# A Mamba-style layer between two feed-forward layers: scan tiles of 2 states x 64 channels instead of 4 states x 128 channels

## The reference, cut to what matters

```python
h  = layernorm(layernorm(x)) * norm_w + norm_b
xz = h @ Win;  x_ssm, z = split(xz, 2)          # 512 channels each
x_ssm = silu(conv4(x_ssm) + conv_b)
dt = softplus(x_ssm @ dt_w + dt_b);  A = -exp(A_log)
Bt = x_ssm @ Bp;  Ct = x_ssm @ Cp               # 64 states each
def step(state, inp):                           # over 512 tokens
    dA = exp(dt_t[:, :, None] * A[None])
    state = state * dA + (dt_t * x_t)[:, :, None] * B_t[:, None, :]
    y_t = einsum('bds,bs->bd', state, C_t)
y = (ys + x_ssm * D) * silu(z)
out = x + y @ Wout
```

## Time and profile before

| | |
|---|---|
| median of 3 runs | 6116.61 us |
| profiled execution, own time | 6156.25 us |
| its span | 6154.4 us |
| PE matmul busy | 5423.4 us (88%), 86664 instructions |
| POOL busy | 5101.6 us (83%) |
| DVE busy | 4829.4 us (78%) |
| ACT busy | 4068.8 us (66%) |
| mean granted TensorE clock | 0.948 of full |
| DMA packets, bytes | 650457, 1095.40 MB |

### The profile page before, as it was taken

One profiled execution on the slowest core, in us unless ns is written; L12 is line 12 of the kernel. 1 busy time (PEld: TensorE's weight loads), 2 busy tenths in 40 slices (PEclk: granted clock), 3 DMA queues, 4 the chain that ended last, 5 costly groups with the idle time before them and its releaser, 6 DMA issues.

```text
span 6154.4 us, 207624 instructions
## 1 busy us (share of the span) xinstructions
PE 5423.4 (88%) x86664; PEld 3375.6 (55%) x86664; DVE 4829.4 (78%) x4323; ACT 4068.8 (66%) x6785; POOL 5101.6 (83%) x2326
## 2 busy tenths in 40 slices
PE   5888889888898988899888998888988889898887
PEld 2455555555565555555555565555655556555554
DVE  0679787787887878788787887878778788797996
ACT  3767576666766667576675766657666676766664
POOL 0779798887988879798797988979888798897996
PEclk9899999999999999999999999999999999999999
DMA  5566665666656666666665656656566666655553
GB/s 132 199 153 222 145 212 171 169 202 153 208 156 188 202 157 208 155 187 199 161 209 150 197 194 157 210 143 209 176 170 206 148 213 156 190 189 142 191 179 112
DMA packets 650457, 1095.40 MB, mean 178 GB/s; under 512 B 302817, under 2 KB 336386, under 8 KB 583938
## 3 DMA queue, kind: packets, MB, share of 16 engines
q1 hardware_dynamic: 649474, 1081.40, 60.9%
HBM read 875.74 MB, written 205.52 MB: 176 GB/s over the span
## 4 chain that ended last, share of the span: by engine, by line
POOL 52%; issue 23%; PE 10%; SPq 6%; DMA 5%; DVE 1%; ACT 1%; POOLq 1%; DVEq 0%; ACTq 0%
POOL H L602 49%; SPq L303 6%; DMA Cb<-scratch_c 4%; PE pUB L687 3%; PE Y L713 3%; DVE H L567 1%; POOL lnv L616 1%; POOL dto L620 1%; PE pP L642 1%; PE pP L648 1%; SPq L289 1%; PE pP L635 1%; POOLq L601 0%; DMA Bd<-scratch_diag 0%; POOL X L626 0%
## 5 line engine op out<-in xcount | busy, mean ns | idle before, releaser
L567 DVE TENSOR_TENSOR_SCAN H<-dA,pUB 128x512 f32<-128x512 f32 x4096 | 4698.3, 1203 | 1108.8 <-PE pUB L687 1061.6
L602 POOL TENSOR_TENSOR H<-H,Cb 128x1024 f32<-128x1024 f32 x2048 | 4814.8, 2387 | 824.1 <-DVE H L567 815.7
L435 ACT ACTIVATE dA<-DT,w_negA 128x512 f32<-128x512 f32 x4096 | 2615.3, 710 | 1134.5 <-DVE H L567 1121.6
L687 PEld LDWEIGHTS pUB<-Bd,UT 64*64 64x64 f32 x65536 | 1975.6, 136 | 1560.5 <-issue 1547.5
L687 PE MATMUL pUB<-Bd,UT 64*64 64x128 f32 x65536 | 2303.3, 277 | 556.5 <-DMA Bd<-scratch_diag 247.1
L713 PE MATMUL Y<-H,w_ident 64*64 64x512 f32 x16384 | 2026.9, 605 | 69.4 <-POOL H L602 63.1
L713 PEld LDWEIGHTS Y<-H,w_ident 64*64 64x64 f32 x16384 | 660.6, 137 | 658.2 <-issue 649.4
L435 ACT ACT_TABLE_LOAD x224 | 287.4, 1283 | 4.0
L408 ACT ACTIVATE absv<-pP,w_dt_b 128x512 f32<-128x512 f32 x64 | 44.0, 687 | 358.3 <-PE pP L648 358.3
L635 PE MATMUL pP<-hT,w_Win 128*128 128x512 f32 x512 | 264.4, 641 | 16.0 <-ACT uto L423 12.7
L648 PE MATMUL pP<-U,w_dt_w 128*128 128x512 f32 x512 | 270.9, 655 | 3.4 <-ACT zo L399 3.4
(11 more groups left out here) (85 smaller groups left out, 2350.3 us busy)
## 6 DMA issues: line engine op xcount, KB each, us to landing
Cb<-scratch_c SPq DMA_DIRECT2D x512, 1024.0 KB, 5.5
Bd<-scratch_diag SPq DMA_DIRECT2D x512, 512.0 KB, 4.5
scratch_diag<-blank SPq DMA_DIRECT2D x512, 256.0 KB, 5.9
scratch_z<-zo SPq DMA_DIRECT2D x64, 256.0 KB, 6.3
scratch_dt<-dto SPq DMA_DIRECT2D x64, 256.0 KB, 6.4
scratch_ut<-uto SPq DMA_DIRECT2D x64, 256.0 KB, 7.4
DT<-scratch_dt SPq DMA_DIRECT2D x64, 256.0 KB, 5.3
UT<-scratch_ut SPq DMA_DIRECT2D x64, 256.0 KB, 6.6
```

The source lines that it names most:

```text
L435: last = nc.scalar.activation(dA[:, n % DAR, j, :], DT[:, k, :], ACT.Exp, scale=c["negA"][:, k, GS * blk + j:GS * blk + j + 1])
L567: last = nc.vector.tensor_tensor_scan(H[:, n % HR, 2 * i + j, :], dA[:, n % DAR, 2 * i + j, :], pUB[:, i, :].rearrange("p (t s) -> p s t", ...
L602: nc.gpsimd.tensor_tensor(h[:, j:j + 2, :], h[:, j:j + 2, :], Cb[:, blk % 2, j:j + 2, :], ALU.mult).then_inc(times_c, 1)
L687: last = nc.tensor.matmul(out, UT[rows, k, j * P + h * HP:j * P + h * HP + HP], Bd[rows, blk % 2, i, j * P:(j + 1) * P].rearrange("p (t s) ...
```

## The change

The unit keeps its size (128 partitions x 4 scans x 512), but a partition now stands for one of 64 channels and one of two pairs of states. The four quarters of 32 partitions are (channels 0-31, states 0-1), (channels 0-31, states 2-3), (channels 32-63, states 0-1), (channels 32-63, states 2-3). The four scans of a unit are two channel tiles (`j // 2`) by two states (`j % 2`). So:

- `force` makes 32 matmuls for a half unit (4 x 4 quarters x 2), with 32 weights' columns and 128 moving columns each, in 64x32 tiles, where there were 16 in 64x64 tiles.
- `add_states` is one call for each pair, placed behind `force(n+1, 1)` at even n. Its weights `sel` are four 32x32 identities below one another, so the product over 64 partitions adds the two pairs of states. A pair takes 16 matmuls of 512 columns in 64x32 tiles, where it took two calls of 8 in 64x64 tiles.
- `skip_over` takes 8 matmuls of 128 rows x 32 columns twice per sequence instead of 2 of 64x64 four times. It moves to n = 2 and 34.
- `Cb` needs 2 rows of C for each partition instead of 4, so its load halves. C is stored twice, dt is stored twice, and `DT` is loaded at twice the size.
- `store_diagonals` stores one of 8 parts a unit, n = 25 to 32, each 64 partitions x 16 pieces of four numbers.
- The setup loads `A_log` in 32 small transfers instead of 1, and `Win`, `Wout` in 32 pieces instead of 16.

```diff
-SPS = {... "store B": (25,), ...
+SPS = {... "store B": (25, 26, 27, 28, 29, 30, 31, 32), ...
...
+            rates = w["A_log"].rearrange("(q r i) (b p t) -> r p q i b t", q=2 * KI, r=2, b=NBLK, p=2)
+            small += [(alog[(2 * r + par) * QP:(2 * r + par + 1) * QP, q, :].rearrange("p (b t) -> p b t", t=2), rates[r, par, q])
+                      for r in range(2) for par in range(2) for q in range(2 * KI)]
...
+            link(nc.vector.tensor_tensor(c["sel"][:, :], c["ident"][:, 0:QP], c["ident"][:, QP:2 * QP], ALU.add))
+            for part in (2, 3):
+                link(nc.vector.tensor_tensor(c["sel"][:, :], c["sel"][:, :], c["ident"][:, part * QP:(part + 1) * QP], ALU.add))
...
-                rows = dram["c"][bass.ds(b, 1), GS * blk + 1:GS * (blk + 1) + 1, :].rearrange("o s t -> o (s t)")
-                sp.dma_start(Cb[:, seq % 2].rearrange("p s t -> p (s t)"), rows.to_broadcast([P, GS * T])).then_inc(c_in[seq % 2], 16)
+                rows = dram["c"][bass.ds(b, 1), 2 * GS * blk + 1:2 * GS * (blk + 1) + 1, :].rearrange("o (p s) t -> p (o s t)", p=4)
+                rows = rows.unsqueeze(1).to_broadcast([4, QP, 2 * T])
+                sp.dma_start(Cb[:, seq % 2].rearrange("p s t -> p (s t)"), rows).then_inc(c_in[seq % 2], 16)
...
+                j, r = part // 2, part % 2
+                    lo = EL + r * HP * 2 * T + j * HP * GS
+                    spot = dram["diag"][bass.ds(q, 1), lo:lo + NBLK * 2 * EL].rearrange("o (i x) -> (o i) x", x=2 * EL)
+                    spot = spot[:, 0:HP * (2 * T + GS)].rearrange("i (p x) -> p i x", x=2 * T + GS)[:, :, 0:GS]
+                    sp.dma_start(spot, BT[r * HP:r * HP + HP, j, :].rearrange("p (i s) -> p i s", s=GS)).then_inc(d_st, 16)
...
+                for par in range(2):
+                    sp.dma_start(rows[par], dto[:, :]).then_inc(dt_st, 16)
...
-                            last = nc.scalar.activation(dA[:, n % DAR, j, :], DT[:, k, :], ACT.Exp,
-                                                        scale=c["negA"][:, k, GS * blk + j:GS * blk + j + 1])
+                            last = nc.scalar.activation(dA[:, n % DAR, j, :], DT[:, k, j // 2, :], ACT.Exp,
+                                                        scale=c["negA"][:, 2 * k + j // 2, 2 * blk + j % 2:2 * blk + j % 2 + 1])
...
-                            nc.gpsimd.tensor_tensor(h[:, j:j + 2, :], h[:, j:j + 2, :], Cb[:, blk % 2, j:j + 2, :], ALU.mult).then_inc(times_c, 1)
+                            nc.gpsimd.tensor_tensor(h[:, j:j + 2, :], h[:, j:j + 2, :], Cb[:, blk % 2], ALU.mult).then_inc(times_c, 1)
...
-                    for r in range(2):
-                        rows = slice(r * HP, r * HP + HP)
-                        for h in range(2):
-                            side = slice(h * HP, h * HP + HP)
-                            out = pUB[side, i, r * T:(r + 1) * T].rearrange("p (t j s) -> p j t s", j=NJ, s=2)[:, j]
-                            last = nc.tensor.matmul(out, UT[rows, k, j * P + h * HP:j * P + h * HP + HP],
-                                                    Bd[rows, blk % 2, i, j * P:(j + 1) * P].rearrange("p (t s) -> p t s", s=2),
+                    for quarter in range(4):
+                        ch = j * P + i * HP + quarter // 2 * QP
+                        for r in range(2):
+                            rows = slice(r * HP, r * HP + HP)
+                            out = pUB[quarter * QP:(quarter + 1) * QP, i, r * T:(r + 1) * T].rearrange("p (t j s) -> p j t s", j=NJ, s=2)[:, j]
+                            last = nc.tensor.matmul(out, UT[rows, k, ch:ch + QP],
+                                                    Bd[rows, blk % 2, j, :, quarter % 2 * 2:quarter % 2 * 2 + 2],
                                                     start=True, stop=True)
...
+            def add_states(b, n):
+                pe.wait_ge(times_c, at(2 * (GN * b + n + 2)))
                 pe.sem_inc(pe_go, 1)
+                for j in range(2):
+                    for q in range(4):
+                        for r in range(2):
+                            rows = slice(r * HP, r * HP + HP)
+                            last = nc.tensor.matmul(Y[r][q * QP:(q + 1) * QP, :], c["sel"][rows, :], H[rows, (n + q // 2) % HR, q % 2 * 2 + j, :],
+                                                    start=False, stop=(n % HALF == HALF - 2 and j == 1))
+                last.then_inc(summed, 2)
...
-                    if n % 2:
-                        other(b, n, close, proj, ffn)
-                    if scan and n % 2 == 0 and n:
-                        add_states(b, n - 2, 1)
+                    other(b, n, close, proj, ffn)
+                    if scan and n % HALF == 2:
+                        skip_over(b, n // HALF)
                     if scan and n + 1 < GN:
                         force(b, n + 1, 1)
-                    if n % 2 == 0:
-                        other(b, n, close, proj, ffn)
-                    if scan and n % 2:
-                        add_states(b, n - 1, 0)
+                    if scan and n % 2 == 0 and n:
+                        add_states(b, n - 2)
```

More of the change, by code:

```diff
@@ L14 @@
 HP = P // 2
+QP = P // 4
 GS = 4
@@ L101, in _ @@
                 sp.dma_start(dst, src).then_inc(k_big, 16)
-            for k in range(KI):
-                for r in range(2):
[L104 to L110, removed]
+            for tile in range(KI):
+                for q in range(4):
+                    side, ch = q * QP, tile // 2 * 2 * P + q * HP + tile % 2 * QP
+                    sp.dma_start(c["Win"][:, :, DI + tile * P + side:DI + tile * P + side + QP],
+                                 w["Win"][:, DI + ch:DI + ch + QP].rearrange("(k p) m -> p k m", p=P)).then_inc(k_big, 16)
+                    sp.dma_start(c["Wout"][side:side + QP, tile, :], w["Wout"][ch:ch + QP, :]).then_inc(k_big, 16)
+            sp.wait_ge(k_big, (4 + 8 * KI) * 16)
+            sp.wait_ge(k_small, (10 + 8 * KI) * 16)
         @block.gpsimd
@@ L120, in _ @@
         def _(act):
[L121 removed]
+            act.wait_ge(k_small, (10 + 8 * KI) * 16)
             nc.scalar.activation(wabs[:, :, :], wk[:, :, :], ACT.Abs).then_inc(k_abs, 1)
@@ L698, in skip_over @@
                 pe.sem_inc(pe_go, 1)
                 for r in range(2):
-                    rows, side = slice(r * HP, r * HP + HP), slice(k % 2 * HP, k % 2 * HP + HP)
-                    last = nc.tensor.matmul(Y[r][side, :], c["diagD"][rows, k, rows], U[rows, k, :] if k < 2 else U2[rows, k - 2, :],
-                                            start=True, stop=False)
-                last.then_inc(skip, 1)
-            def add_states(b, n, half):
-                pe.wait_ge(times_c, at(2 * (GN * b + n + 1) + half + 1))
-                pe.sem_inc(pe_go, 1)
-                for j in (2 * half, 2 * half + 1):
-                    for r in range(2):
-                        rows = slice(r * HP, r * HP + HP)
-                        for i in range(2):
-                            last = nc.tensor.matmul(Y[r][i * HP:i * HP + HP, :], c["ident"][rows, rows], H[rows, (n + i) % HR, j, :],
-                                                    start=False, stop=(n % HALF == HALF - 2 and j == GS - 1))
-                if half:
-                    last.then_inc(summed, 2)
+                    for q in range(4):
+                        k, lo = 2 * pr + q // 2, q % 2 * HP + r * QP
+                        last = nc.tensor.matmul(Y[r][q * QP:(q + 1) * QP, :], c["diagD"][:, k, lo:lo + QP],
+                                                U2[:, k - 2, :] if pr else U[:, k, :], start=True, stop=False)
@@ L833, in step @@
                         force(b + 1, 0, 1)
-                    if n % 2 == 0:
-                        other(b, n, close, proj, ffn)
-                    if scan and n % HALF == 1:
-                        skip_over(b, n - 1)
-                        skip_over(b, n)
-                    if scan and n % 2:
-                        add_states(b, n - 1, 0)
+                    if scan and n % 2 == 0 and n:
+                        add_states(b, n - 2)
+                    if close and n == 0:
+                        add_states(b - 1, GN - 2)
             steps(pe, step)
```

74 lines of the change are left out of this document (36 added, 38 removed).

## The result

The changed kernel takes **6300.7 us** (median of 4 runs, 6260.7 to 6324.4) for 6118.3 us of the kernel before beside it: a ratio of 1.0292, 95% interval 1.0234 to 1.0351. The forecast was 5570 us, with 5420 to 5860 as its range. The profiled execution took 6285.92 us.

What follows compares the result with a forecast made beforehand. POOL was taken to set the floor: 318.7 us busy plus 16.3 idle make 335 a sequence; 229.5 + 15 x 335 + 349 = 5603.5 us of span, 5605 own time, times 0.9936 gives 5570 us, range 5420 to 5860.

Steps and rivals of the forecast that it cites:

- the array step: On TensorE, a round of tiles costs its columns, not its instructions: 107 ns for eight tiles in `force`.
- Rivals 3 and 4: Eight tiles don't run side by side, 7470 us, chance 0.05; matmuls are paced one by one, 6600 us, chance 0.03.
- The first scan: End of the setup: added small transfers make the first scan come 32 us later, at 229.5 us.
- A store: Diagonal stores on SP: with half the pieces, each takes 1.5 us of SP, one a unit.
- The long stall on `Bd`: The wait for the load of `Bd` behind eight diagonal stores goes: -16.7 us a sequence.
- `Cb` at half size ... all far ahead of their use: 0: Loads and stores of `Cb`, C, dt and `DT`: all far ahead of their use, cost 0.
- `force`: 32 instructions become 64, in 8 rounds as before: 0: `force` calls on TensorE: twice the instructions in the same 8 rounds cost 0.
- rival 2: TensorE is late through instructions or clock: 22 us a sequence, 5900 us, range 5650 to 5950, chance 0.20.
- 1.1 + 1.9 + 1.1 = 4.1 us fit into 4.5 ... Cost 0: Later place of `add_states` between two `force` calls: cost 0, up to 0.5 us a pair if POOL lags.
- all shapes on ACT, DVE and POOL at 0: ACT, DVE and POOL run the same instructions with the same shapes: cost 0.

Runs made afterwards that it cites:

- e1: The kernel before with only the eight diagonal stores spread, one a unit at n = 25 to 32: 5955.66 us, ratio 0.972.
- e3: The changed kernel with the C rows loaded in four transfers of 32 partitions instead of one: 6030.79 us, ratio 0.9859.
- e8: The kernel of e5 with the C rows in one transfer of 2 x 64 x 1024 instead of two: 7318.52 us, ratio 1.1958.
- e5: The changed kernel laid out in halves of 64 channels, tiles 64 wide or more, C rows in two transfers, C and dt stored once: 6342.11 us, ratio 1.0363.
- e4: The changed kernel with its force products in 64x64 tiles, part of the products wrong: 5962.04 us, ratio 0.9733.
- e13: The kernel of e1 with a one-token matmul added ahead of each force matmul, tiles as before: 7141.52 us, ratio 1.1671.
- e6: The changed kernel with the edits of e3 and e4 together, part of the products wrong: 5752.02 us, ratio 0.9404.
- e14: The kernel of e3 with the Y sum ahead of the second force call, other pieces of even units behind it: 6077.17 us, ratio 0.9928.
- e9: The kernel of e1 with the diagonals stored in pieces of four numbers: 5913.44 us, ratio 0.9664.
- e12: The kernel of e1 with two long-fulfilled semaphore waits ahead of each force matmul: 6458.44 us, ratio 1.0543.

## Why the prediction was wrong

*Right, nearly:* the array step. A round with eight tiles costs little more than one with four did (an undisturbed call of 64 takes 1.19 us, 1.1 forecast), and the Y sum's busy time is 1112.3 us (about 1030 forecast). Over all 2048 calls, the broken ones and those at half clock among them, `force` is busy 2711.3 us for 2303.3. Rivals 3 and 4 are out. The first scan comes at 231.0 us (229.5 forecast). A store takes SP 0.69 us, less than half of the 1.5 forecast. The long stall on `Bd` is gone; spreading alone was worth 166 us or 11 a sequence (e1) for the 16.7 forecast, as part of the wait moved to unit 32.

*The term "`Cb` at half size ... all far ahead of their use: 0"* failed, and cost 270 us (e3 undoes it). I counted bytes, not how many DMA engines carry them. In the 5 us shown above the 16 engines are busy 0.23 of their time, 3.7 engines, at 69 GB/s. At that rate 512 KB take 7.6 us of a pair's 9.3, and the next `Bd` stands behind them: it lands after 6.6 us instead of 4.5. With the outermost dimension at 2 (e8) 2.2 engines are busy and it costs 976 us, and transfers of one row to 32 or 64 partitions each (e3, e5) leave no wait of POOL on `Cb`. The cause is thus the transfer's shape. The Trainium skill ("DMA: Bandwidth & Descriptors", Why a DMA increments its semaphore by 16 and not by 1) says that a transfer uses as many engines as the largest number up to 16 that divides the slowest dimension, other than 1, of both its patterns: 4 here (4 and 128), 2 in e8 (2 and 128). The 3.7 and the 2.2 agree. Had I weighed that rule, the term would not have been 0.

*The term "`force`: 32 instructions become 64, in 8 rounds as before: 0"* failed too, and cost up to 339 us (e4 undoes it, with the wider tiles). It priced the array and left the longer list at nothing: that was rival 2's mechanism, to which I gave 0.20. Rival 2's price for it, 22 us a sequence or 330 in all, agrees with the 339 in the sum only, and that is partly luck: I had put 0.3 us on each of 75 blocks of instructions, and what came is about 24 late ones a sequence of 1.3 us each. What misled me was the earlier trace rows, 62 waits over a whole run: they were too few to look dear, and I took the price of a block for a flat one. It is not flat. Of the blocks that come every 7.9 us 1 in 12 was late (63 waits to 726 packets), and of those every 4.5 us about 3 in 10 are (384 to 1237, each 1.3 us in the mean). The late ones fall into `force`, the densest part of the list (64 matmuls in 1.19 us, for the Y sum's 32 in 1.99), and DVE waits for it. e13 shows the pauses with the tiles unchanged; that it is the block's arrival that ends them rests on their times beside queue 8. The Trainium skill ("Runtime: NRT & Kernel Launch", Instruction fetch mechanics) calls the crossing of a 16-KB block "mostly hidden"; here 509 us of TensorE's idle time aren't, and the measurement decides.

*The rest, 5752 - 5570 = 182 us,* is there even without both causes (e6): 345 us a full sequence for 335, 319 the last one for 298.6 (in its profiled execution, 30 us above its median). The one other place that was tried for the Y sum isn't better (e14). For the last sequence the step can be named: "1.1 + 1.9 + 1.1 = 4.1 us fit into 4.5 ... Cost 0", said of a force call, the Y sum and the force call that DVE needs next. From e6, the last sequence and 14 us of it, and the timeline there:

```profile
5403.50:5722.50 319.00, 242.94 (x5139) 158.58 (x5133) 288.25 (x258) 171.54 (x280) 294.69 (x128) 0.90 0.38 116
5562.00:5576.00 14.00, 11.20 (x224) 6.80 (x220) 12.83 (x12) 7.41 (x12) 13.13 (x6) 0.78 0.32 92
```

```profile
5561.78 1.98 PE L702 MATMUL pUB<-Bd,UT 64*64 64x128 f32 x32 [1.08 <-DVE H L582]
5563.69 2.40 PE L728 MATMUL Y<-H,w_sel 64*32 64x512 f32 x32
5566.02 2.06 PE L702 MATMUL pUB<-Bd,UT 64*64 64x128 f32 x64
5567.32 9.07 DVE L582 TENSOR_TENSOR_SCAN H<-dA,pUB 128x512 f32<-128x512 f32 x8 [1.17 <-PE pUB L702]
...
5572.02 1.99 PE L702 MATMUL pUB<-Bd,UT 64*64 64x128 f32 x32 [1.12 <-DVE H L582]
```

From the start of the first call to the scan that the last of the three releases it is 5567.32 - 5561.78 = 5.5 us, not 4.1, and DVE waits 1.17. TensorE has less to do, is idle ahead of `force`, and is granted 0.78 of its clock in these 14 us, 0.90 in the whole sequence, for 0.99 before. The call takes 1.98 us in place of 1.14 (that is 1.2 GHz for most of it, as at the branch in the earlier trace rows) and the Y sum 2.40 for 1.99. In the waits of the last sequence, before and in e6, that is the whole gap of 20 us:

```profile
DVE H L567 <- PE pUB L687: 11.4, 27, 2.6
...
DVE H L582 <- PE pUB L702: 31.5, 29, 1.5
```

The chain that ended last agrees: in this sequence POOL has 1.5% of it, for 40.8% before, and DVE, `force` and the Y sum take turns with 42.9, 26.7 and 19.4%. The Y sum's gain is thus partly given back as clock. This is argued from the trace; no run held the clock and kept the order.

For the 10 us of each full sequence the cause stays open. I priced all shapes on ACT, DVE and POOL at 0, and one group of DVE in e6 did take longer, 160.6 us for 90.5 before, 70 in all:

```profile
L591 DVE SCALAR_TENSOR_TENSOR ev<-ev,absv 128x512 f32<-128x512 f32 x64 | 160.6, 2510 | 80.6 <-ACT ev L433 80.6
```

That can explain part of e6's time but nothing of the changed kernel's own, where the same group takes 79.2 us, less than before.

The sum, 5570 + 182 + 549 for both causes together = 6301, closes because the 182 are what was left.

## What to carry to other kernels

When a change cuts work into smaller instructions, count the instructions per us of the densest stretch as well as the array's rounds: with late blocks already visible in the profile's "issue" waits, more of them fall on the path. Price a transfer by its outermost dimension before its bytes. A win that needs neither was here all along: spreading eight stores over eight units and writing pieces of four numbers gave 3.4% (e9).

## What was not expected of the hardware

- The same 512 KB in one transfer of 4 rows or in four transfers of one row: 270 us over the kernel. In one of 2 rows or in two of one row: 976 us.
- Sixteen more instructions in a call of 32 matmul records add 0.4 us (1.12 to 1.53 in the mean, e12), although they are waits that have long been fulfilled. (The trace has 240782 instructions for 208014 in e1, 16 more for each of 2048 calls.)
- One DVE instruction of unchanged shape (`ev<-ev,absv`) takes 1414 ns in the mean before, 1237 in the changed kernel, 2510 in e6 and 672 in e12. POOL's busy share doesn't order them: it is 88% in e6 and 87% in e9, where the mean is 1262 ns. What does is open.
